# An attention kernel whose TensorE turns each sequence's values at another place: ahead of the product with the probabilities

## The reference

```
h = tokens(x)                                    # 64 x 93 x 128
q, k, v = causal 3-tap convolutions of projections of norm(h)   # 8 heads of 64
P = softmax(q k^T * scale - slope * |i - j|, causal)            # per head, 93 x 93
h = h + (P v) @ wout.T
h = h + top-2 of 16 experts, each expert's answer being a mean over its tokens
```

## Time and profile before

| | |
|---|---|
| runs, median (lowest to highest) | 760.93 us (758.69 to 762.31) |
| profiled execution, its own time | 763.01 us |
| its span, first to last instruction | 761.1 us |
| mean granted TensorE clock | 0.98 |
| instructions | 21415 |
| `weigh` (L576), first to last | 70.5 to 606.5 us |
| `turn_values` (L566), first to last | 63.5 to 600.1 us |

### The profile page before, as it was taken

How to read it: one execution, slowest core, us unless ns; L and a number is a source line. 1 busy time by engine, 2 the same in 40 slices (tenths; PEclk the granted TensorE clock), 3 DMA queues, 4 the chain that set the end, 5 groups by cost and what they waited for, 6 DMA issues and landing times.

```text
span 761.1 us, 21415 instructions
## 1 busy us (share of the span) xinstructions
PE 713.1 (94%) x6672; PEld 639.9 (84%) x6672; DVE 566.7 (74%) x1579; ACT 608.2 (80%) x2022; POOL 376.2 (49%) x390
## 2 busy tenths in 40 slices
PE   8589999999999999999999999988897788999996
PEld 8478888888898888889898888877776678999994
DVE  3166777888778887878778887888875468888875
ACT  4557898989898999989898999778676676899960
POOL 4652435666557566666557566545343464122200
PEclk9989999999999999999999999999999989999996
DMA  6432134242222122221221121120224012122205
GB/s 205 134 83 62 42 97 139 69 130 53 72 53 53 49 55 51 53 74 51 67 55 53 48 58 53 32 71 14 59 56 172 22 49 76 51 64 69 62 19 162
DMA packets 44274, 54.01 MB, mean 71 GB/s; under 512 B 13651, under 2 KB 31251, under 8 KB 43696
## 3 DMA queue, kind: packets, MB, share of 16 engines
q1 hardware_dynamic: 30048, 38.84, 17.9%
q0 software_dynamic: 12544, 12.87, 6.3%
q10 hardware_dynamic: 1616, 1.48, 0.6%
HBM read 42.69 MB, written 10.26 MB: 70 GB/s over the span
## 4 chain that ended last, share of the span: by engine, by line
PE 43%; DVE 25%; ACT 19%; issue 7%; DMA 3%; POOL 2%; DVEq 0%; ACTq 0%; SPq 0%; POOLq 0%
ACT prob L826 12%; DVE qkv L1000 5%; PE psTP L452 5%; DVE qkv L1003 5%; PE psTP L454 4%; PE psTP L453 4%; PE psTP L723 4%; PE psSO L723 4%; DVE prob L1116 4%; PE psTP L524 3%; PE psSO L543 3%; DMA x_raw<-in_x 3%; PE psSO L668 3%; ACT qkv L803 3%; PE psSO L576 2%
## 5 line engine op out<-in xcount | busy, mean ns | idle before, releaser
L1349 POOL DMA_INDIRECT expert_rows<-hn,slot x128 | 167.7, 1310 | 63.0 <-issue 31.9
L826 ACT ACTIVATE prob<-psSO,rmin 93x93 f32<-93x93 f32 x512 | 151.9, 355 | 8.2 <-DVE rmin L1086 8.0
L1282 POOL TENSOR_TENSOR x_lo<-x_raw,x_hi 128x752 fp32r<-128x752 f32 x64 | 115.3, 1802 | 51.9 <-ACT x_hi L795 51.4
L1000 DVE SCALAR_TENSOR_TENSOR qkv<-psTP,taps,qkv 128x368 f32<-128x368 f32 x192 | 112.6, 586 | 20.9 <-ACT qkv L803 20.4
L803 ACT ACTIVATE qkv<-psTP,taps 128x372 f32<-128x372 f32 x192 | 113.1, 589 | 11.4 <-PE psTP L454 10.7
L1003 DVE SCALAR_TENSOR_TENSOR qkv<-psTP,taps,qkv 128x364 f32<-128x364 f32 x192 | 114.5, 597 | 6.8
L452 PE MATMUL psTP<-x_hi,wtok_hi 128*128 128x376 f32 x256 | 97.5, 381 | 2.8 <-POOL x_lo L1282 2.8
L826 ACT ACTIVATION_READ_ACCUMULATOR prob<-psSO,rmin 93x1 f32 x512 | 98.7, 193 | 0.0
L454 PE MATMUL psTP<-x_hi,wtok_lo 128*128 128x376 f32 x256 | 86.3, 337 | 0.0
L453 PE MATMUL psTP<-x_lo,wtok_hi 128*128 128x376 f32 x256 | 86.2, 337 | 0.0
L452 PE MATMUL psTP<-xnT_hi,wqkv_hi 128*128 128x372 f32 x192 | 77.6, 404 | 7.7 <-DVE qkv L1003 6.6
(11 more groups left out here) (198 smaller groups left out, 1711.9 us busy)
## 6 DMA issues: line engine op xcount, KB each, us to landing
x_raw<-in_x SPq DMA_DIRECT2D x64, 376.0 KB
w1s<-in_w POOLq DMA_DIRECT2D x8, 512.0 KB
w<-in_w SPq DMA_DIRECT2D x4, 1024.0 KB
out<-resid SPq DMA_DIRECT2D x16, 160.0 KB, 2.5
xsE<-expert_rows SPq DMA_DIRECT2D x36, 64.0 KB, 1.9
xs<-expert_rows SPq DMA_DIRECT2D x36, 64.0 KB, 1.8
xs<-expert_rows POOLq DMA_DIRECT2D x36, 64.0 KB, 2.1
expert_rows<-hn,slot POOLq DMA_INDIRECT x128
```

What stands on the lines that cost most here:

```text
L826: i = nc.scalar.activation(prob[:, a, hh, :], psS[:NT, a, hh * NT:(hh + 1) * NT], ACT.Exp, bias=rmin[:, a, hh:hh + 1], scale=-1.0, accum_o ...
L1000: nc.vector.scalar_tensor_tensor(dst[:, :, 1:NT], src[:, :, 0:NT - 1], taps[:, k, 1:2], dst[:, :, 1:NT], ALU.mult, ALU.add).then_inc(tap1_ ...
L1282: nc.gpsimd.tensor_tensor(x_lo[u][:, 0:PIECE], x_raw[u][:, :], x_hi[u][:, 0:PIECE].bitcast(F32), ALU.subtract)\
L1349: nc.gpsimd.indirect_dma_start(rows, bass.IndirectOffsetOnAxis(slot[1 - u][:, c:c + 1], 0), hn[1 - u][:, c % GB, :], None)\
```

## The change

`turn_values` is called ahead of `weigh` in every slot of the attention stage, in place of behind projection block 3s+1. Operands, banks, semaphores and the other engines' instructions stay as they are.

```diff
                     if f.tok:
                         tok_taps(t, s, 0, 1)
+                    if f.attn:
+                        turn_values(t, u, f, s, n)
                     if prev:
                         weigh(s, n)
                     if q is not None and s == 0:
                         turn_quad(q)
                     if f.proj:
                         proj(t, u, f, 3 * s + 1)
-                    if f.attn:
-                        turn_values(t, u, f, s, n)
                     if f.tok:
                         tok_taps(t, s, 1, 1)
```

## The result

The changed kernel takes 774.88 us (median; 774.71 to 775.81), the kernel before beside it 760.71: a ratio of 1.0188, with a 95% interval of 1.0171 to 1.0204. It is slower by 14.2 us, where 13.6 was forecast. The profiled execution took 774.88 us with a span of 773.2.

What follows compares the result with a forecast made beforehand. A chain from TensorE's weighing and projection block through ScalarE and VectorE to the next scores was taken to bound the kernel beside TensorE. Terms 3.7 + 3.2 + 4.7 + 0.7 + 1.3 = 13.6 us gave 774.5 us, range 767 to 780.

Steps and rivals of the forecast that it cites:

- TensorE's share misleads: Whole kernel: TensorE is busy 94% of the span, yet hand-overs to ScalarE and VectorE form a chain with 0.13-0.17 us spare.
- Price of the four transposes: Ahead of `weigh` and projection block 3s+1: the transposes make both end 0.44 us later in each slot.
- Entry of the weighing: Start of `weigh`: going over to products on 64 columns costs 0.10 us, taken as unchanged behind a short transpose.
- both bounds: Entry of `weigh`: its 0.10 us may vanish, giving 770.3 us, or double, giving 778.7.
- lower bound of 770.3: Entry of `weigh` becomes free: each of 42 priced places costs 0.10 us less, -4.2 us in all.
- Slots 0, 1, and 2 with 3: Full steps: slot 0 pays 0.27 us, slot 1 pays 0.31, slots 2 and 3 pay 0.44 for both together.
- half case: Rival: slots 2 and 3 have room once slot 0 has paid, others pay; 8.2 us, 769; chance 15%.
- The first steps: Four first steps: slot 3 hands over to slot 0 with about slot 1's spare, so 0.30 us there, 4 x 0.30.
- Steps 15 to 17: Price only where `tap2` closely follows its projection block: three of 12 slots at 0.26 us, 0.7 us; between nothing and 5.3.
- Step 18: Three slots without projections, where the copy closely follows `weigh`: nearly full price, 3 x 0.43 = 1.3 us.
- What would show it: Profile after: scores 0.15 us behind scaling in slots 0 and 1, step 35.3 us, TensorE idling ahead of scores dozens of times.

Runs made afterwards that it cites:

- pair with the exponentials first: ScalarE's eight exponentials in one piece ahead of copy and tap, in the kernel before and in the changed one: 750.58 and 751.12 us, ratios 0.9873 and 0.9868.
- kernel with slot 2 alone: Kernel before with the four transposes moved ahead of the weighing in slot 2 only, the other three slots unchanged: 767.35 us, ratio 1.0067.
- kernel with only the block late: Kernel before with the transposes moved between the weighing and projection block 3s+1: 771.76 us, ratio 1.0132.
- mixed version: Kernel before with ScalarE's eight exponentials in one piece where there are projections, old order in step 18: 748.33 us, ratio 0.9834.

## Why the prediction was right

- *TensorE's share misleads; the hand-overs bound the kernel.* Right, and shown by the pair with the exponentials first.
- *Price of the four transposes, 0.44 us.* Right for the full steps: doubling them adds 0.43 to 0.44 us in each of slots 0 to 2. In step 18, where TensorE comes to them from a wait, they and the entry of the weighing take 0.61 us and not 0.53.
- *Entry of the weighing.* I had taken it as unchanged and let both bounds stand. After, it starts 0.53 us behind the first of four transposes (315.26 to 315.79), of which three spacings of 0.11 are theirs: 0.20 for the last, so 0.09 for the entry, against the 0.10 before. The cost is the same, within 0.01 us, whether a long product or a short transpose stands ahead. The lower bound of 770.3, which needed the entry to become free, falls. The rule of the Trainium skill, TensorEngine Tiling (Array Packing), section Tiling Modes (Key Properties), that a change of the tiling mode drains TensorE, agrees with an entry that costs as much at either place; the traces show that cost and not where it comes from.
- *Slots 0, 1, and 2 with 3.* 0.25, 0.33, 0.46 and 0.02 us measured one by one, against 0.27, 0.31, 0.44 and 0. The half case (slots 2 and 3 find room once slot 0 has paid) is refuted: the single prices add up to 1.06, and the whole change costs 1.04. These terms carry the forecast: 8 x 1.02 = 8.2 us for the eight full steps, and 8.3 measured.
- *The first steps.* The term that was too small. Up to sequence 15 the change cost 4.4 us (127.86 to 132.23); my terms give 3.3 for them (4 x 0.31 + 3 x 0.27 + 4 x 0.30). Slots 2 and 3 of these steps had been priced at 0.30 a step without a row read for it. The kernel with slot 2 alone costs 0.43, 0.48 and 0.44 us in steps 4, 5 and 6, so half of the shortfall is that slot 2 pays in full from the start; the rest stays open.
- *Steps 15 to 17.* 0.9 for 0.7 (three times 0.26 is 0.8, to be exact). The size was about right by luck, for the reason was wrong: the price was put down to the projection block's tap, and the kernel with only the block late pays nothing there.
- *Step 18.* 1.0 for 1.3, and not put together as forecast. Three slots were to pay 0.43 each. From weighing to weighing, slots 0, 1 and 2 take 7.63, 6.76 and 7.17 us before and 7.62, 7.29 and 7.65 after: slot 0 pays nothing, the other two pay 0.53 and 0.48. One error is hidden in part by the other.
- *What would show it.* The scores start 0.15 us behind the scaling in slots 0 and 1; the step is 35.4 us. Two signs came out weaker than announced. TensorE's idle time was to rise to about 1.2 us a step, and the profile shows 0.62, for its busy time went up by 6.5 us (719.6, not within a few us of 713) without any work added, as told above. And the idling ahead of the scores, announced dozens of times, shows 26 times after and 8 times before; those of 0.15 us or less in the full steps are not listed. The lines have us in total, times, and the longest; first before, then after:

```profile
PE psSO L538 <- DVE prob L1116: 3.6, 8, 1.2
```

```profile
PE psSO L538 <- DVE prob L1116: 6.9, 26, 1.1
```

That 13.6 us came so near to 14.2 is helped by luck: the first steps were put 1.1 too small and step 18 0.3 too large, steps 15 to 17 have the right size for a wrong reason, and the span itself scatters by more than any of them. What the runs bear out is the mechanism in the full steps, which make over half of the price.

## What to carry to other kernels

An engine that is 94% busy can still be one link of a chain. Before moving work on it, measure at each hand-over how long the result lies before the receiver takes it: 0.04 us means that the receiver waits and a delay goes on down the chain, less what a later link has to spare (0.13 and 0.17 us in slots 1 and 0); 0.8 us, as in slot 3, is what can be spent. And where a long independent piece (here four exponentials) stands in an engine's fixed order behind something that comes late from another engine, try moving it ahead: here that gained 10.9 us, where an earlier hand-over gained nothing.

## What the runs showed of the hardware that I had not expected

With the exponentials first in all steps, TensorE idles about 1.2 us in slots 0, 1 and 2 of step 18 in front of the output projection, in both kernels of the pair. In the changed one, and not in the other, the granted clock fell in this stretch. Sequence 59 to 62, first of the kernel before with the edit, then of the changed one with it, then of the mixed version (columns as in the earlier trace rows):

```profile
564.84:587.55 22.71, 17.47 (x199) 14.85 (x200) 10.81 (x42) 14.08 (x67) 11.96 (x12) 1.00 0.27 96
```

```profile
566.35:590.65 24.30, 19.11 (x200) 16.41 (x199) 10.34 (x38) 14.04 (x67) 11.96 (x12) 0.93 0.22 79
```

```profile
562.67:583.67 21.00, 18.00 (x199) 14.87 (x200) 10.44 (x42) 14.19 (x67) 11.98 (x12) 1.00 0.28 103
```

The mean clock of 0.93 means that part of the stretch ran at the lower of the two levels, 1.2 GHz instead of 2.4. The output projection at 568.35 shows it: 1.74 us where the same instruction takes 1.11 elsewhere.

```profile
568.35 1.74 PE L668 MATMUL psSO<-wout,attnT 128*93 128x128 f32 x8 [1.13 <-ACT attnT L881]
...
577.41 1.11 PE L668 MATMUL psSO<-wout,attnT 128*93 128x128 f32 x8 [1.19 <-ACT attnT L881]
```

The two kernels differ there by little more than where the transposes stand, and I made no run to tell whether that decides it or the phase does; it is one profile of each. It is also a part of why the profiled spans of the pair are 4.1 us apart (747.7 and 751.8) where the medians are 0.5 apart: this stretch gives 1.6 us. Another 1.9 us lie between the weighings of sequences 47 and 59, where the granted clock of the changed one fell as well, to a mean of 0.98, and that of the other stayed at 1.00:

```profile
465.89:566.35 100.46, 93.30 (x919) 79.46 (x918) 87.29 (x262) 79.47 (x318) 46.54 (x49) 0.98 0.21 61
```
